# Light network and routing in one stage of a four-part transformer kernel: descent, search and one-hots between the groups' operations

## The reference, cut to what matters

```python
def coor_descent(s, k, n_iters, eps):          # eps = 1, n_iters = 50
    def step(ab, _):
        a, b = ab
        a = eps * (logk - logsumexp((s + b) / eps))
        b = -relu(s + a)
        return ((a, b), None)
    ...                                        # b starts as -s
    return exp((s + a + b) / eps)
light_out = feed_forward(x, light_...)         # 512 -> 256 -> 512, gelu, every token
s = einsum('bnd,d->bn', x, routing_token)
scores = coor_descent(s, 512 * 9 / 8, 50, 1.0)
sel_scores, sel_idx = top_k(scores, 512)
routed_out = feed_forward(x[sel_idx], heavy_...)   # 512 -> 2048 -> 512
return light_out + zeros.at[sel_idx].set(routed_out * sel_scores)
```

## Time and profile before

| | us |
|---|---|
| median of 3 runs | 4095.25 (4093.11 to 4096.59) |
| the profiled execution | 4095.83 |
| its span | 4093.3 |
| light stage, first product to last result | 234.5 |
| from there to the heavy stage's first instruction | 212.7 |
| heavy stage | 429.9 |

### The profile page before, as it was taken

One profiled execution on the slowest core, in us unless ns is written; L12 is line 12 of the kernel. 1 busy time (PEld: TensorE's weight loads), 2 busy tenths in 40 slices (PEclk: granted clock), 3 DMA queues, 4 the chain that ended last, 5 costly groups with the idle time before them and its releaser, 6 DMA issues. The chain is left out here.

```text
span 4093.3 us, 56822 instructions
## 1 busy us (share of the span) xinstructions
PE 3568.4 (87%) x16277; PEld 2413.9 (59%) x16277; DVE 2724.6 (67%) x5471; ACT 1492.1 (36%) x5333; POOL 1918.5 (47%) x1784
## 2 busy tenths in 40 slices
PE   8599999999837999999996999999999696249998
PEld 4355555555426777777774555555555475227776
DVE  3477777777687677677673677777776443366665
ACT  0365666666400111111111666666666221201110
POOL 0255555555401777767773556555555232012332
PEclk9799999999955999999997999999999898569999
DMA  5455545454312666666664456555653555000111
GB/s 159 129 147 151 144 141 166 143 143 138 110 42 69 169 165 161 163 170 159 161 168 105 126 137 169 147 152 138 166 153 113 188 216 208 12 21 6 20 21 18
DMA packets 323211, 523.11 MB, mean 128 GB/s; under 512 B 59257, under 2 KB 104121, under 8 KB 322553
## 3 DMA queue, kind: packets, MB, share of 16 engines
q1 hardware_dynamic: 290808, 443.79, 36.6%
q0 software_dynamic: 32256, 77.65, 10.1%
...
## 5 line engine op out<-in xcount | busy, mean ns | idle before, releaser
L691 ACT ACTIVATE t_pr<-ps,t_negmax 128x154 f32<-128x154 f32 x2048 | 867.9, 547 | 529.4 <-DVE t_negmax L471 528.7
L414 POOL TENSOR_TENSOR t_pr<-t_pr,t_inv 128x616 f32<-128x616 f32 x512 | 642.6, 1256 | 616.3 <-DVE t_inv L486 613.6
L494 DVE COPY t_pTm<-ps 128x512 f32<-128x512 f32 x512 | 349.9, 683 | 315.0 <-PE ps L735 310.7
L785 PE MATMUL ps<-t_xnT,t_wq 128*128 128x512 f32 x1024 | 505.2, 617 | 19.1 <-ACT t_qT L612 18.9
L806 PE MATMUL ps<-t_wo,t_oT 128*128 128x512 f32 x1024 | 497.9, 610 | 7.8 <-DVE t_xs L503 6.6
L734 PEld LDWEIGHTS ps<-ident,t_pr 128*128 128x128 f32 x2048 | 317.9, 204 | 296.1 <-issue 258.0
L691 ACT ACTIVATION_READ_ACCUMULATOR t_pr<-ps,t_negmax 128x1 f32 x2048 | 472.1, 230 | 0.0
L471 DVE TENSOR_REDUCE t_negmax<-ps 128x4 f32<-128x616 f32 x512 | 403.1, 787 | 30.1 <-PE ps L722 29.6
L734 PE MATMUL ps<-ident,t_pr 128*128 128x128 f32 x2048 | 334.4, 286 | 51.7 <-DVE t_pTm L494 36.1
L722 PE MATMUL ps<-t_kst,t_stack 98*128 98x154 f32 x2048 | 340.1, 289 | 15.0 <-DMA t_stack<-t_q_low 13.2
L785 PEld LDWEIGHTS ps<-t_xnT,t_wq 128*128 128x128 f32 x1024 | 176.9, 192 | 229.4 <-issue 203.2
...
## 6 DMA issues: line engine op xcount, KB each, us to landing
...
t_stack<-t_q_low SPq DMA_DIRECT2D x512, 64.0 KB, 2.0
...
t_kst<-kst_dram SPq DMA_DIRECT2D x128, 235.8 KB
...
```

The source lines that it names most:

```text
L414: pool.tensor_tensor(p, p, inv[:, v, :].unsqueeze(1).to_broadcast([P, KEYS, HG]), ALU.mult).then_inc(s["normed"], 1)
L494: dve.tensor_copy(pTm[:, g % 2, :, t * P:(t + 1) * P], ps[:, 4, :].rearrange("p (h n) -> p h n", h=HG)).then_inc(s["pTm"], 1)
L691: op = act.activation(pr[:, u % 4, :, h], ps[:, 2 * (u % 2) + h // 2, at:at + KEYS], ACT.Exp, bias=negmax[:, u, h:h + 1], accum_out=total[ ...
L785: mm = pe.matmul(ps[:, A_BANK, :], wq[:, k, n * P:(n + 1) * P], xnT[:, k, :], start=(k == 0), stop=(k == DC - 1))
```

## The change

`light_phase` and `routing_phase` become one, `mixed_phase`, in one block; the computation of the light network stays as it was.

- The descent is written otherwise. With e = exp(s - shift) a step is cap = sum(min(e, cap)) / k, so that exponentials and logarithm are taken once a round of seven steps (7 rounds = 49 steps), and the sum over partitions is made on DVE: spread the column over 32 (`wide`), transpose 32 x 32 blocks, reduce (`over_rows`).
- The search takes three bits a step with seven candidates at once (11 steps), its sums over partitions again on DVE.
- All that DVE does for the routing is a generator, `routing()`; `advance(m)` puts the next m of its operations into DVE's list, and the table `paces(n)` says how many stand before each of the light group's operations. Groups 0 to 6 hold a round of the descent each, 7 to 10 the search and the positions, 11 to 15 the 64 one-hots, 13 a group.
- PE multiplies the one-hots in the same groups, 5 and 8 between the light products; the fourth set of transposes moves behind the first two output products, and the transposes share three PSUM banks in turn instead of four.
- The cast to h's high part moves from DVE to ACT, which also gets the exponentials and logarithms with the loads of their tables.
- The ring of one-hots has 14 buffers for 4. SP sends z 0 first, the scores and the heavy biases ahead of z 1, and the heavy weights in eight parts of 1 MB in groups 3 to 10. `heavy_phase` stays, but for the count it waits for.

```diff
-def light_phase(nc, a, scr, c, out):
+def mixed_phase(nc, a, scr, c, out):
 
     LC = LIGHT // P
+    R = P // B
+    C = SEQ // R
+    LOGK = math.log(EFF_K)
+    ROUND, CLIP = 7, 20.0
+    ROUNDS = (ITERS - 1) // ROUND
+    DIGIT, WAYS = 3, 8
+    STEPS = 11
+    RING = 14
+    SIDE = 3
...
+            sp.dma_start(z[0][:], rows(scr["xs"], 0)).then_inc(s["z_in0"], 16)
+            sp.dma_start(w1_in[:], a["light_w1"].rearrange("(k p) n -> p k n", p=P)).then_inc(s["w_in"], 16)
             with nc.allow_non_contiguous_dma(reason="biases by partition"):
                 sp.dma_start(gam[:], a["light_gamma"].rearrange("(k p) -> p k", p=P)).then_inc(s["w_in"], 16)
                 sp.dma_start(b1[:], a["light_b1"].rearrange("(k p) -> p k", p=P)).then_inc(s["w_in"], 16)
-            sp.dma_start(w1_in[:], a["light_w1"].rearrange("(k p) n -> p k n", p=P)).then_inc(s["w_in"], 16)
             sp.dma_start(w2_in[:], a["light_w2"].rearrange("(k p) n -> p k n", p=P)).then_inc(s["w_in"], 16)
             sp.dma_start(b2[:], a["light_b2"].partition_broadcast(P)).then_inc(s["w_in"], 16)
-            for n in range(NG):
+            sp.wait_ge(s["flat"], 1)
+            sp.dma_start(scr["scores"].rearrange("(t p) -> t p", p=P), flat[:]).then_inc(s["flat_out"], 16)
+            sp.dma_start(xs[0][:], rows(scr["x1"], 0)).then_inc(s["xs_in0"], 16)
+            sp.wait_ge(s["flat_out"], 16)
+            sp.dma_start(sco[:], scr["scores"].rearrange("(q j) -> q j", j=C)).then_inc(s["s_in"], 16)
+            with nc.allow_non_contiguous_dma(reason="biases and scales by partition"):
+                sp.dma_start(c["hb1"][:], a["heavy_b1"].rearrange("(k p) -> p k", p=P)).then_inc(c["hw_in"], 16)
+                sp.dma_start(c["hgam"][:], a["heavy_gamma"].rearrange("(k p) -> p k", p=P)).then_inc(c["hw_in"], 16)
+            sp.dma_start(c["hb2"][:], a["heavy_b2"].partition_broadcast(P)).then_inc(c["hw_in"], 16)
+            for n in range(1, NG):
...
+                if 3 <= n < 3 + DC:
+                    k = n - 3
+                    sp.dma_start(c["hw1"][:, k, :], a["heavy_w1"][k * P:(k + 1) * P, :]).then_inc(c["hw_in"], 16)
+                if 7 <= n < 7 + DC:
+                    k = n - 7
+                    sp.dma_start(c["hw2"][:, 4 * k:4 * k + 4, :], a["heavy_w2"][k * 4 * P:(k + 1) * 4 * P, :].rearrange(
+                        "(f p) d -> p f d", p=P)).then_inc(c["hw_in"], 16)
...
+            def over_rows(columns, out, scale=None, done="step"):
+                linked()
+                v = wide[:, 0:columns.shape[1], :]
+                if scale is None:
+                    link(dve.tensor_copy(v, columns.unsqueeze(2).to_broadcast([P, columns.shape[1], R])))
+                else:
+                    link(dve.tensor_scalar(v[:, 0, :], ones[:], columns, scale, ALU.mult, ALU.mult))
+                linked()
+                vT = wideT[:, 0:columns.shape[1], :]
+                link(dve.transpose(vT.rearrange("p w r -> p (w r)"), v.rearrange("p w r -> p (w r)")))
+                linked()
+                if done == "step":
+                    link(dve.tensor_reduce(out, vT, AX, ALU.add))
+                else:
+                    dve.tensor_reduce(out, vT, AX, ALU.add).then_inc(s[done], 1)
...
+            def shifted(i):
+                linked()
+                reached(dve, s["na"], i)
+                link(dve.tensor_scalar(shift[:], na[:], smax[:], None, ALU.min))
+                linked()
+                dve.tensor_scalar(sbv[:], sco[:], shift[:], CLIP, ALU.subtract, ALU.min).then_inc(s["shifted"], 1)
+                dve.tensor_scalar(above[:], na[:], shift[:], CLIP, ALU.subtract, ALU.min).then_inc(s["shifted"], 1)
...
+                for i in range(ROUNDS):
+                    dve.wait_ge(s["exped"], 2 * i + 2)
+                    for n in range(ROUND):
+                        linked()
+                        link(dve.tensor_scalar(kept[:], ex[:], cap[:], 0.0, ALU.min, ALU.add, accum_out=part[:]))
+                        yield
+                        yield from over_rows(part[:], cap[:], 1.0 / EFF_K, "step" if n + 1 < ROUND else "capped")
+                    dve.wait_ge(s["logged"], i + 1)
+                    dve.tensor_scalar(na[:], lse[:], shift[:], None, ALU.add).then_inc(s["na"], 1)
+                    yield
+                    if i + 1 < ROUNDS:
+                        yield from shifted(i + 1)
...
+                for i in range(STEPS):
+                    linked()
+                    link(dve.tensor_tensor(lower[:], u[:].unsqueeze(1).to_broadcast([P, WAYS - 1, C]),
+                                           cand[:, 1:WAYS].bitcast(F32).unsqueeze(2).to_broadcast([P, WAYS - 1, C]),
+                                           ALU.is_lt))
+                    yield
+                    linked()
+                    link(dve.tensor_reduce(count[:], lower[:], AX, ALU.add))
+                    yield
+                    yield from over_rows(count[:], total[:, 1:WAYS])
...
+                    link(dve.scalar_tensor_tensor(kind[:], total[:], float(ROUTED), cand[:].bitcast(F32), ALU.is_lt,
+                                                  ALU.mult))
+                    yield
+                    linked()
+                    link(dve.tensor_reduce(edge[:], kind[:], AX, ALU.max))
...
+                        link(dve.tensor_tensor(cand[:], edge[:].bitcast(I32).to_broadcast([P, WAYS]),
+                                               digit[:, i + 1, :], ALU.bitwise_or))
+                        yield
...
+                for j in range(C):
+                    reached(dve, s["hot_mm"], j - RING + 1)
+                    dve.tensor_scalar(hot[:, j % RING, :], slots[:], pos[:, j:j + 1], None,
+                                      ALU.is_equal).then_inc(s["hot"], 1)
+                    yield
+                dve.wait_ge(s["hot_mm"], C)
+                dve.tensor_copy(found[:], ps[0:2 * B, SIDE, :]).then_inc(s["found"], 1)
...
-                dve.wait_ge(s["h"], LC * n + f + 1)
-                reached(dve, s["y_mm"], TG * n)
-                high_of(dve, hT[0][:, f, :], h[:, f, :]).then_inc(s["h_high"], 1)
...
+            def paces(n):
+                if n < ROUNDS:
+                    return (13, 7, 2, 2, 2, 1, 1, 0, 0, 4 if n + 1 < ROUNDS else 1)
+                if n < 11:
+                    return (11, 5, 2, 2, 2, 2, 2, 1, 1, 2) if n < 10 else (9, 4, 2, 2, 2, 1, 1, 1, 0, 1)
+                return (4, 2, 1, 1, 1, 1, 1, 1, 1, 0) if n < NG - 1 else (4, 2, 1, 1, 1, 1, 1, 1, 0, 0)
...
+                pace = paces(n)
+                advance(pace[0])
                 split_h(n, 0)
+                advance(pace[1])
+                z_low(n + 1, 0)
+                advance(pace[2])
...
+            def exponentials(i):
+                act.wait_ge(s["shifted"], 2 * i + 2)
+                act.activation(ex[:], sbv[:], ACT.Exp).then_inc(s["exped"], 1)
+                act.activation(cap[:], above[:], ACT.Exp).then_inc(s["exped"], 1)
+            def logarithm(i):
+                act.preload_act_table_set("natural_log_exp_and_others")
+                act.wait_ge(s["capped"], i + 1)
+                act.activation(lse[:], cap[:], ACT.Ln).then_inc(s["logged"], 1)
...
+                    act.wait_ge(s["h"], LC * n + f + 1)
+                    reached(act, s["y_mm"], TG * n)
+                    act.copy(hT[0][:, f, :], h[:, f, :]).then_inc(s["h_high"], 1)
...
+                if n < ROUNDS:
+                    logarithm(n)
+                if n + 1 < ROUNDS:
+                    exponentials(n + 1)
...
+                reached(pe, s["z_low"], DC * n + k - 2)
...
+            def found_rows(first, last):
+                for j in range(first, last):
+                    pe.wait_ge(s["hot"], j + 1)
+                    pe.matmul(ps[0:2 * B, SIDE, :], vals[:, j, :], hot[:, j % RING, :], start=(j == 0),
+                              stop=(j == C - 1)).then_inc(s["hot_mm"], 1)
...
+                z_turn(n + 1, 0)
+                z_turn(n + 1, 1)
+                z_turn(n + 1, 2)
+                if n >= 11:
+                    found_rows(hots(n), hots(n) + HOTS[0])
+                outer(n, 0, 0)
+                outer(n, 1, 0)
+                z_turn(n + 1, 3)
+                outer(n, 0, 1)
+                outer(n, 1, 1)
+                outer(n, 2, 0)
+                outer(n, 3, 0)
+                if n >= 11:
+                    found_rows(hots(n) + HOTS[0], hots(n + 1))
+                outer(n, 2, 1)
+                outer(n, 3, 1)
+                if n == ROUNDS:
+                    pe.wait_ge(s["made"], MADE)
+                    pe.wait_ge(s["flat"], 1)
+                    pe.wait_ge(s["na"], ROUNDS)
+                    for b in range(B):
+                        mm = pe.matmul(ps[:, SIDE, b:b + 1], pick[:, b, :], na[:], start=True, stop=True)
+                    mm.then_inc(s["na_mm"], 1)
...
-            light_phase(nc, a, scr, c, out)
...
-            routing_phase(nc, a, scr, c)
```

(1 more changed line is left out.)

393 lines of the change are left out of this document (202 added, 191 removed).

## The result

The changed kernel takes 3931.43 us (median of 4 runs, 3929.78 to 3934.01), the kernel before on the same chip 4095.92: a ratio of 0.960, 95% interval 0.958 to 0.962, 164.5 us less. I had forecast 3942 us and a gain of 154.0; the time lies in the forecast's own range, 10.6 us under the forecast. The profiled execution has a span of 3930.0 us.

What follows compares the result with a forecast made beforehand. PE paced the light stage, a serial dependent chain the routing; merged, DVE would bound groups 0 to 6. 447.2 us before became 2.8 + 285.1 + 5.3 = 293.2, gain 154.0: 3942 us, own range 3922 to 3965, with rivals 3902 to 3988.

Steps and rivals of the forecast that it cites:

- The exit: After the last light store: one block's exit, 5.3 us, stays; the routing chain's new end, hidden behind that store, costs nothing.
- The start: Before the merged stage: light weights 0.6 us later, seven routing operations before DVE's first group; 2.8 us delay.
- Sum 6.9 + 7.5 + 0.9 = 15.3 us, already over PE's 14.7: Groups 0 to 6: DVE's light share, seven descent steps and round's end exceed PE's time, so DVE becomes the bound.
- The descent term: Groups 0 to 6: four linked DVE operations take 1.07 us a step, seven steps 7.5 us a group.
- The light term: DVE's ten light operations at 0.68 to 0.69 us each make 6.9 us a group.
- the port: DVE's SBUF operations wait beside POOL's additions: 0.7 us a group in 0-6, 1.6 in 7-9, 0.9 in 11-15.
- Groups of 14.7 would refute the DVE sum: Sign to check in the profile of groups 0 to 6, which were forecast at 16.7 us with DVE nearly always busy.
- The search step: Groups 7 to 10: a three-bit step is eight DVE operations, 3.2 us; eleven steps are 35 us.
- rival 3: Merged stage: PE's clock falls as it idles in pieces, slower than before, 4121 us; chance 0.03.
- 14.7 + 3.0 + 0.9 = 18.6: Groups 11 to 15: PE's light group, 13 one-hot products and port collisions, 18.6 us a group.
- Rival 1: Merged stage: PE paces throughout, DVE's waits hidden, no collisions; gain 191.6, 3904 us; chance 0.14.
- Rival 2: Every group: port or in-order waiting costs 2.5 us more than forecast, 3982 us; chance 0.18.

Runs made afterwards that it cites:

- both moves: Changed kernel with fewer routing operations between zT_low 0 and result 1 (groups 0-10), all 13 one-hots ahead of next zT_low 0 (groups 11-15): 3906.43 us.
- the kernel with the shorter chain: Changed kernel with DVE routing operations moved out from between zT_low 0 and result 1, same number per group: 3915.28 us.
- the one-hots ahead: Changed kernel with all 13 one-hots of groups 11 to 15 made between result 3 and the next group's zT_low 0: 3921.7 us.
- the serial run: Changed kernel with its rewritten routing, but all routing work laid behind the last light group, none between groups: 4001.86 us.

## Why the prediction was right, and where it was right by luck

**The joint.** The exit, 5.3 (5.4), and the tail of the routing hidden behind the last store are as worked out. The edges, as the earlier trace rows:

```profile
3493.30 0.38 SPq L1486 DMA_DIRECT2D out_rows<-l_xs  x1
...
3494.78 0.17 DVE L1689 CAST c_heavy_rows<-l_rows_f 128x16 int32<-128x16 f32 x1
3498.63 0.76 DVE L69 CAST h_w_high<-c_hw 128x512 fp32r<-128x512 f32 x2 [3.68 <-PEq L58]
```

The start, 2.8 us forecast and 3.1 measured, is right by luck. I had laid the delay at DVE's first group, behind seven routing operations; it stands ahead of PE's first product, and the first routing operation starts only at 3217.42:

```profile
3212.10 2.28 DVE L1722 TENSOR_TENSOR l_w_low<-l_w_in,l_w_high 128x1024 fp32r<-128x1024 f32 x1
...
3215.05 1.12 PE L1828 MATMUL ps<-ident,l_z 128*128 128x128 f32 x4 [8.13 <-DVE l_zT_low L1728]
```

The weights come 1.8 us later in the stage for the forecast's 0.6, the operation above that makes their low part takes 2.28 us for 1.22, now beside POOL's additions, and the fourth transposes wait for the first zT_low, since they share three banks and no longer four.

**Groups 0 to 6** are where the sum missed, 116.9 for 107.9, and there the step that failed is "Sum 6.9 + 7.5 + 0.9 = 15.3 us, already over PE's 14.7". What DVE needs for the 32 routing and ten light operations can be read from the two kernels without POOL's additions, as the group's time less DVE's waits. The waits in a group with the changed kernel's paces (15.03 us), then in one with both moves (14.01 us):

```profile
3270.48 0.69 DVE L1723 TENSOR_TENSOR l_zT_low<-ps,l_zT_high 128x512 fp32r<-128x512 f32 x1 [0.32 <-ACT l_zT_high L1781]
...
3277.37 0.69 DVE L1734 TENSOR_TENSOR l_xs<-ps,l_xs 128x512 f32<-128x512 f32 x1 [1.14 <-PE ps L76]
```

```profile
3289.09 0.69 DVE L1734 TENSOR_TENSOR l_xs<-ps,l_xs 128x512 f32<-128x512 f32 x1 [0.45 <-PE ps L76]
```

They leave 13.57 and 13.56 us, where the sum had 15.3; that is under PE's 13.67, not over it. The descent term holds: in the changed kernel's group 3 the clipped sum starts at 3283.88, 3284.95 and 3286.01, 1.07 us a step. The light term is over-sized: ten operations were counted by their durations of 0.69, while the trace spaces them by 0.60, and less beside a small operation, which leaves some 5.2 us for the ten instead of 6.9 (13.6 less 7.5 and 0.9). On top of the 13.6 come DVE's waits, 1.2 us a group in the changed kernel and 1.5 without POOL for the forecast's 0.7, and the port, 0 to 0.6 for 0.7. So the sum was 1.7 us too long and the waits were 0.5 too short; together with the port that is the 1.3 us a group, 9.0 in seven. The waits are mostly the chain of zT_low 0 to result 1, which I hadn't seen: with the same operations in other places they fell by 1.0 us (15.03 to 14.01 without POOL). So in the changed kernel DVE was not the bound. It is one in the kernel with both moves: there a group of 14.46 us has no wait of DVE, and is its 13.6 and 0.9 for operations held up beside POOL. I had written "Groups of 14.7 would refute the DVE sum": the kernel with the shorter chain ran the same DVE work in 14.45, which refutes the size of the sum.

**Groups 7 to 9** came out at 61.3 for 61.2 by errors that cancel. The search step is shorter than forecast. In the kernel without POOL's additions, two starts of its first comparison:

```profile
3327.59 0.62 DVE L1597 TENSOR_TENSOR l_lower<-l_u,l_cand 128x448 f32<-128x448 f32 x1
...
3332.23 0.62 DVE L1597 TENSOR_TENSOR l_lower<-l_u,l_cand 128x448 f32<-128x448 f32 x1
```

4.64 us with three light operations of 0.60 between is 2.8 a step for the forecast's 3.2, and the light share is smaller too. Against that stand DVE's waits, for which my sum had no term here (7.4 us in the three groups, 5.6 of them for PE at results), and the port; POOL's additions cost 2.4 us a group for 1.6, but that figure takes in what I gave a chance of 0.03 as a mechanism of loss: the clock. The changed kernel in group 7, DVE and then PE:

```profile
3340.50 0.90 DVE L1611 SCALAR_TENSOR_TENSOR l_kind<-l_total,l_cand 128x8 f32<-128x8 f32 x1
3341.32 0.68 DVE L1739 TENSOR_TENSOR l_xs<-ps,l_xs 128x512 f32<-128x512 f32 x1
...
3342.05 0.50 PE L74 MATMUL ps<-l_w_high,l_hT_high 128*128 128x512 f32 x1 [3.26 <-DVE l_xs L1739]
...
3343.28 0.72 PE L74 MATMUL ps<-l_w_high,l_hT_high 128*128 128x512 f32 x1 [0.26 <-DVE l_xs L1739]
```

About 1.2 us after PE's wait of 3.26 us for result 0 has ended, its products stand in the trace at 0.72 and then 0.63 us where they were 0.50 and 0.39, the clock of the group is 0.92, and PE is busy 16.40 us for 14.73 in the same group of the kernel without POOL's additions, where it stays at 1.00. I forecast 1.00 throughout; rival 3 is real in small, at some 1.5 us a group, in three groups of 16. POOL is not needed for it: without its additions groups 8 and 9 still ran at 0.91. This also makes the stretch scatter: with identical code groups 7 to 10 took 77.6, 74.6, 75.1, 75.8 and 72.9 us in five profiles, and the clock fell in three of these groups in four of the profiles and in two in the fifth, the shortest. Differences of under 5 us there prove nothing alone.

**Groups 11 to 15** (forecast 14.7 + 3.0 + 0.9 = 18.6, measured 18.45) have two terms right, products 3.00 and port 0.87, and a base that was wrong in a way that cancelled. I let 14.7 stand with its 1.7 us of waits; the new order makes it 13.67, and the one-hots in the chain put 0.9 back (17.58 without POOL, 16.67 with the one-hots ahead).

**The rivals.** Rival 1, PE pacing throughout, had a gain of 191.6; both moves reached 186.0, but PE's floor was 13.67 and not 14.7, and groups 7 to 9 stayed at 16.2 to 17.5 us, so only the number is near. Rival 2's mechanism, a late DVE operation in one queue delaying PE, is the chain; its price was 1.0 us a group and not 2.5. No wait of PE ended on ACT, no DMA became a bound, and the serial run shows that the code gains 89 us without any overlap, for which I had no term; since the sum took the whole 212.7 us as gone and priced the new operations one by one, it didn't need one.
